# A third step taken ahead in an attention-over-pairs kernel, with the scores of all ahead steps as one run before the first regular step

## The chip, the core and the metric

The kernel runs on one core of a Trainium2 chip. The metric is the device time of one execution in microseconds (us), lower is better, given as the median of several runs.

## What is computed

For 1,024 samples, 33 embedding rows of 128 values each are gathered from 33 tables by `ids`. All 528 pairs of fields are multiplied elementwise, each product goes through a 128x128 attention layer with relu, and its dot product with the sample's own `gnn` vector is the pair's score:

```python
inner = x[:, row] * x[:, col]                       # row, col: all pairs of 33 fields
fm = relu(einsum('bpd,ad->bpa', inner, attn_W) + attn_b)
attn = softmax(einsum('ba,bpa->bp', gnn, fm), axis=1)
out = einsum('bp,bpd->bd', attn, inner) * 100.0
z = concatenate([gnn, out], axis=1)
h = concatenate([z, gnn], axis=1)
h = maximum(h @ W_top1 + b_top1, 0.0)
h = maximum(h @ W_top2 + b_top2, 0.0)
y = h @ W_top3
```

## The kernel before

**Tiles and steps.** The samples form T = 8 tiles of 128, and a tile 32 steps of 4 samples. A pair is a field and a distance of 1 to 16, so with 16 fields repeated at the end (33 + 16) one access pattern gives all 16 x 33 = 528 pairs. A regular step S has 4 x 528 = 2,112 columns, in five chunks of 416 or 424 that fill halves of PSUM slots of two banks.

**Who does what in step S.** DVE multiplies (`product`, L464). ACT rounds a part of the product to fp32r (`round_inner`, L355), and DVE forms the rest (`rest_of_inner`, L470: product minus the rounded part). PE computes `hidden(S)`: the first one to three chunks ("native", L627) as fp32 matmuls, each two records in the trace, the others ("split") as three fp32r matmuls (L634 to L636) that need both parts. ACT applies bias and relu, two chunks to an instruction (L347), into one of three `fm` buffers. Every second step PE runs `reduce_steps` (L673): the scores of two steps, 16 small matmuls (32 records), whose weights put each of four groups of samples on its own 32 columns of the array; they accumulate in one PSUM tile over the whole tile of samples. `reduce_steps` raises `s_red` once per run, and a relu into an `fm` buffer waits until the step three before is reduced.

**The steps ahead.** At the start the 33 gathers of the first tile (GpSimd, L320, in chunks of 8 fields, the fifth of 1) come in one after another. While fields 16 to 32 are still on the way, pairs whose two fields lie among the first 16 (8 distances x 8 fields = 64 pairs) can be done. A step ahead has S < 0 and takes 32 samples at once: 32 x 64 = 2,048 columns, four native chunks of 512. There are two (S = -2, -1), for 64 samples, which are those of the regular steps 0 to 15. These steps, S < SHORT = 16, are "short": 4 x (528 - 64) = 1,856 columns in four chunks of 464. The scores of the two ahead steps (64 matmuls of 64 columns, 128 records) come after hidden(0), as those of any pair of steps do.

**What sets the order.** Each engine runs its own list in program order; there is no scheduler. PE's loop (L740) issues hidden(S), then the jobs of step S (`jobs_of`): transposes of gathered fields (`transpose_x`, L682), the `fields` and `mlp` matmuls of the tile before, and at even S the scores of S-2 and S-1. In step -1 the jobs are the transposes of chunks 2, 3 and 4 of the first tile; those of the next tile stand at steps 18, 20, 22, 24 and 26 of each tile. ACT's loop (L410) issues the first relu of step S, the rounding of step S+2, the other relus, then the evacuations of what was transposed (`evacuate_xt`, L386) and the repeats of the first 16 fields (`repeat`, L376; for the first tile after steps -2 and -1). DVE makes the ahead products, waits for all five evacuations and both repeats, makes product(0), and then in iteration S the rest of step S+1 and product(S+3).

**PSUM slots.** `hidden` pairs of chunks, `x_t`, `fields` and `mlp` units take the slots of a ring of RING = 3 in the order of the list `units` (L121); `claim` (L613) waits until the unit three places before has been taken out. A short step has two hidden units, two full steps have five together, three of them in the even one.

**Queues.** SP stores the gathered rows to DRAM for tile 0 after hidden(1) (L281), then for tile 1, and GpSimd's gathers of a later tile wait for the store of the tile before and for its transposes (L317, L318).

Of the kernel before, what the change touches and what calls it, by code (L numbers as in the profile page):

```python
# [12 lines left out]
def afm_tower(nc, gnn, ids, tables, w1, b1, w2, b2, w3, attn_w, attn_b, out):  # L13
# [4 lines left out]
    K = (F - 1) // 2  # L18
# [5 lines left out]
    ALL = T * STEPS  # L24
# [6 lines left out]


    AHEAD, AHEAD_SAMPLES = 8, 32
    BEGIN = -2
    SHORT = -BEGIN * AHEAD_SAMPLES // GROUPS
    AHEAD_PAIRS = AHEAD * AHEAD
    NEAR = AHEAD * (F - AHEAD)
# [5 lines left out]
    FU = 8  # L43
    XJ = -(-F // FU)
# [12 lines left out]
    def edges(S):  # L57

        if S < 0:
            return list(range(0, AHEAD_SAMPLES * AHEAD_PAIRS + 1, 512))  # L60
        if S < SHORT:
            return list(range(0, LEFT + 1, LEFT // 4))
        return EDGES[S % 2]

    def chunks(S):
        return len(edges(S)) - 1

    SPLIT = max(edges(S)[-1] - edges(S)[NATIVE[S]] for S in range(ALL))
    INNER_BUFS, HI_BUFS, FM_BUFS = 4, 3, 3
# [2 lines left out]
    FIELDS_AT = (7, 10, 13, 16)  # L72
    XT_AT = (18, 20, 22, 24, 26)
    FIRST_REPEAT_AT = {-2: 0, -1: 1}
    MLP_AT = (19, 21, 23)
    QUIET = 2
    MAX_AT, EXP_AT, INV_AT, SCALE_AT, TURN_AT = 1, 2, 2, 3, 4
# [2 lines left out]
    PART_END = [STEPS * (t + 1) for t in range(T - 1)] + [ALL - FN, ALL]  # L80
# [7 lines left out]
    def jobs_of(S):  # L88
        t, s = divmod(S, STEPS)
        jobs = []  # L90
        if s in FIELDS_AT and t > 0:
            jobs.append(("fields", t - 1, FIELDS_AT.index(s)))
        if S == -1:
            jobs += [("x_t", 0, c) for c in range(2, XJ)]
        if s in XT_AT and 0 < t + 1 < T:
            jobs.append(("x_t", t + 1, XT_AT.index(s)))
        if s in MLP_AT and t > 0:
            jobs.append(("mlp", t - 1, MLP_AT.index(s)))
        if S in LAST_FIELDS_AT:
            jobs.append(("fields", T - 1, LAST_FIELDS_AT.index(S)))  # L100
        return jobs


    CHUNK_LIST = [(S, c) for S in range(BEGIN, ALL) for c in range(chunks(S))]
    CHUNK_NO = {chunk: n for n, chunk in enumerate(CHUNK_LIST)}
    PAIR_OF = [CHUNK_LIST[n:n + 2] for n in range(0, len(CHUNK_LIST), 2)]

    def hidden_by(S):

        return CHUNK_NO[S, chunks(S) - 1] + 1  # L110

    def relus_by(S):

        return CHUNK_NO[S, chunks(S) - 1] // 2 + 1

    def pairs_of_steps(S):

        return (S - BEGIN) // 2


    units = [("x_t", 0, c) for c in range(2)]  # L121
    for S in range(BEGIN, ALL):
        units += [("hidden", n, 0) for n, pair in enumerate(PAIR_OF) if pair[0][0] == S] + jobs_of(S)
# [4 lines left out]
    with ctx:  # L128
# [6 lines left out]
        def sem(name):  # L135
            return ctx.enter_context(nc.semaphore(name))
# [62 lines left out]
        s_fm = sem("fm_ready")  # L199
        s_red = sem("two_steps_reduced")  # L200
# [3 lines left out]
        s_repeat = sem("fields_repeated")  # L204
# [9 lines left out]
        s_xt_out = sem("x_t_evacuated")  # L214
# [7 lines left out]
        def slot(unit):  # L222
            return ring[place[unit] % RING]
# [111 lines left out]
        def _(act):  # L335
            def relu(n):
                act.wait_ge(s_hidden, 2 * n + 2)
                for S, c in PAIR_OF[n]:
                    if c == 0 and S - FM_BUFS >= BEGIN:
                        act.wait_ge(s_red, pairs_of_steps(S - FM_BUFS) + 1)  # L340
                (S0, c0), (S1, c1) = PAIR_OF[n]
                wide = edges(S0)[c0 + 1] - edges(S0)[c0]
                at = [S0 % FM_BUFS * COLS + edges(S0)[c0], S1 % FM_BUFS * COLS + edges(S1)[c1]]
                first = fm[:, 0, 0:1]
                dst = bass.AP(tensor=first.tensor, offset=first.offset + at[0],
                              ap=[first.ap[0], [at[1] - at[0], 2], [1, wide]])
                nc.scalar.activation(dst, slot(("hidden", n, 0))[:, :, 0:wide], ACT.Relu,  # L347
                                     bias=attn_b_sb[:, 0:1]).then_inc(s_fm, 1)

            def round_inner(S):  # L350
                act.wait_ge(s_inner, S - BEGIN + 1)
                if S >= HI_BUFS:
                    act.wait_ge(s_hidden, hidden_by(S - HI_BUFS))
                at, end = native_cols(S), edges(S)[-1]
                nc.scalar.copy(inner_hi[:, S % HI_BUFS, 0:end - at], plain[:, S % INNER_BUFS, at:end]).then_inc(s_hi, 1)  # L355
# [17 lines left out]
            def repeat(t, c):  # L373
                act.wait_ge(s_xt_out, XJ * t + c + 1)
                x = xt[:, t % 2]
                nc.scalar.copy(x[:, :, F + FU * c:F + FU * c + FU], x[:, :, FU * c:FU * c + FU]).then_inc(s_repeat, 1)  # L376
# [33 lines left out]
            for S in range(BEGIN, ALL):  # L410
# [9 lines left out]
                for n in out_now[1:]:  # L420
                    relu(n)
                if S in FIRST_REPEAT_AT:
                    repeat(0, FIRST_REPEAT_AT[S])
                for kind, of, c in jobs_of(S):
# [21 lines left out]
        def _(dve):  # L446
            def product(S):
                if S - INNER_BUFS >= BEGIN:
                    dve.wait_ge(s_hidden, hidden_by(S - INNER_BUFS))
                if S < 0:  # L450
                    pieces = [((S - BEGIN) * AHEAD_SAMPLES, AHEAD_SAMPLES, 0, AHEAD, 1, AHEAD)]
                elif S < SHORT:
                    pieces = [(GROUPS * S, GROUPS, AHEAD, F - AHEAD, 1, AHEAD), (GROUPS * S, GROUPS, 0, F, AHEAD + 1, K - AHEAD)]
                else:
                    pieces = [(GROUPS * (S % STEPS), GROUPS, 0, F, 1, K)]
                end = 0
                for sample, samples, field, fields, near, distances in pieces:
                    x = xt[:, S // STEPS % 2 if S >= 0 else 0, sample:sample + samples, :]
                    a, b = x[:, :, field:field + fields], x[:, :, field + near:field + near + fields]
                    a = bass.AP(tensor=a.tensor, offset=a.offset, ap=[a.ap[0], a.ap[1], [0, distances], a.ap[2]])  # L460
                    b = bass.AP(tensor=b.tensor, offset=b.offset, ap=[b.ap[0], b.ap[1], [1, distances], b.ap[2]])
                    begin, end = end, end + samples * distances * fields
                    dst = plain[:, S % INNER_BUFS, begin:end].rearrange("d (g k f) -> d g k f", g=samples, k=distances)
                    last = nc.vector.tensor_tensor(dst, a, b, ALU.mult)  # L464
                last.then_inc(s_inner, 1)
# [14 lines left out]
                nc.vector.tensor_scalar(high, src, 1.0, None, ALU.mult).then_inc(s_blocks, 1)  # L480

            def row_max(p):
                dve.wait_ge(s_red, pairs_of_steps(PART_END[p]))
                nc.vector.tensor_reduce(neg_max[:, 0:1], scores_v, AX.XY, ALU.max, negate=True).then_inc(s_max, 1)

            def invert_sum(p):
# [82 lines left out]
                .then_inc(s_setup, 1)  # L569
            gnn_block(0)  # L570
            dve.wait_ge(s_xt_out, 2)
            product(-2)
            product(-1)
            dve.wait_ge(s_xt_out, XJ)
            dve.wait_ge(s_repeat, K // FU)
            product(0)
            for S in range(BEGIN, ALL):
                t, s = divmod(S, STEPS)
                if 0 <= S + 1 < ALL:
# [32 lines left out]
        def _(pe):  # L612
# [25 lines left out]
            def block_of(s, j):  # L638
                k = min(s, STEPS - 1 - s)
                at = 34 * k if s == k else 33 * k + 32  # L640
                return gnn_blocks[:, j, at - s:at - s + STEPS]
# [17 lines left out]
                        at = j * PAIRS + h * HALF if S >= SHORT else GROUPS * NEAR + j * HALF  # L659
                        yield s, j, s == 0, scores[I * j:I * j + I, h, 0:HALF], fm[:, S % FM_BUFS, at:at + HALF]  # L660

            def reduce_steps(S0, last_pair=False):
                t, s0 = divmod(S0, STEPS)
                if S0 in PART_END:
                    pe.wait_ge(s_exp, PART_END.index(S0) + 1)
                if S0 == BEGIN or s0 == 0:
                    pe.wait_ge(s_blocks, max(t, 0) + 1)
                pe.wait_ge(s_fm, relus_by(S0 if last_pair else S0 + 1))
                for S in (S0, S0 + 1):
                    if last_pair and S > S0:  # L670
                        pe.wait_ge(s_fm, relus_by(S))
                    for s, j, first, to, columns in scores_of(S):
                        last = nc.tensor.matmul(to, block_of(s, j), columns, start=first, stop=S % STEPS == STEPS - 1,  # L673
                                                skip_group_check=True)
                last.then_inc(s_red, 1)
# [64 lines left out]
            for S in range(BEGIN, ALL):  # L740
                hidden(S)
                for kind, of, c in jobs_of(S):
                    if kind == "fields":
                        fields(of, c)
                    if kind == "x_t":
                        transpose_x(of, c)
                    if kind == "mlp":
                        mlp(of, c)
                if S >= BEGIN + 2 and S % 2 == 0:
                    reduce_steps(S - 2)  # L750
            reduce_steps(ALL - 2, True)
            fields(T - 1, 2)
            pe.wait_ge(s_exp, T + 1)
            keep_clock(6)
# [29 lines left out]
```

## Time and profile before

| | |
|---|---|
| median of 3 runs | 1262.59 us (1262.29 to 1263.55) |
| the profiled execution | 1263.74 us |
| its span in the trace | 1261.6 us |
| mean granted TensorE clock | 0.995 of 2.4 GHz |
| the first regular product begins | 52.56 us |

The rows come from the profiled execution. PE is TensorE's matmuls, PEld its weight loads, DVE VectorE, ACT ScalarE, POOL GpSimd, SP the sync engine. In a timeline a row is a start, a duration, the line and operation, output and inputs, how many instructions are merged, and in brackets the idle time before and what ended it. Ends of matmuls are modelled, so successive rows overlap by 0.1 to 0.4 us; distances between starts are the better measure. In the chain of waits, overlaps are taken out. A granted clock of 1.00 is 2.4 GHz, 0.50 is 1.2 GHz.

### The profile page before, as it was taken

What the parts mean: (1) busy time and instruction counts of PE and PEld (TensorE: products, weight loads), DVE (VectorE), ACT (ScalarE), POOL (GpSimd) and SP (SyncE); (2) the same over time, 40 slices, a digit from 0 to 9 for tenths busy, and PEclk for the clock granted to TensorE, in tenths of its full rate; (3) what the DMA queues carried; (4) which work ended last, traced back from release to release, by engine and by line L of the source; (5) the groups of instructions that cost most, each with busy time, mean ns of one, the idle gap of its engine ahead of it and who ended that gap; (6) DMA issues with size and microseconds to landing.
All of it is one profiled execution on the core that took longest, in us unless ns stands there. A gap on an engine that the chain in (4) does not pass through costs nothing.

```text
span 1261.6 us, 20957 instructions
## 1 busy us (share of the span) xinstructions
PE 1203.4 (95%) x8830; PEld 895.1 (71%) x8830; DVE 1144.7 (91%) x667; ACT 1015.3 (80%) x1035; POOL 450.1 (36%) x270
## 2 busy tenths in 40 slices
PE   1699999999999999999999999999999999999998
PEld 1366776777767777777767777677776777777766
DVE  3399899997999989998899989999799998999994
ACT  1488988778887888879887788878888788887883
POOL 6458588028700485006830088102880000000000
PEclk9799999999999999999999999999999999999999
DMA  3121411311113110131101311031110300011001
GB/s 106 28 91 32 122 32 42 113 41 33 32 28 110 32 30 26 30 112 36 30 20 49 103 30 33 18 111 41 30 34 26 112 18 1 1 30 39 18 9 38
DMA packets 54861, 58.86 MB, mean 47 GB/s; under 512 B 10728, under 2 KB 49136, under 8 KB 53744
## 3 DMA queue, kind: packets, MB, share of 16 engines
q1 hardware_dynamic: 46304, 40.20, 10.4%
q0 software_dynamic: 8448, 17.32, 5.2%
q8 instruction: 70, 1.15, 0.4%
q14 instruction: 23, 0.19, 0.0%
q10 hardware_dynamic: 16, 0.00, 0.0%
HBM read 36.12 MB, written 17.31 MB: 42 GB/s over the span
## 4 chain that ended last, share of the span: by engine, by line
PE 85%; ACT 8%; issue 4%; POOL 3%; DVE 1%; DMA 0%; ACTq 0%; DVEq 0%; POOLq 0%
PE scores L673 20%; PE ring L627 18%; PE ring L634 13%; PE ring L636 12%; PE ring L635 12%; PE ring L696 4%; ACT fm L347 3%; POOL x_rows L320 3%; ACT inner_hi L355 2%; PE ring L682 2%; PE ring L716 1%; ACT exp_pairs L362 1%; PE ring L710 1%; PE ring L706 0%; ACT h L394 0%
## 5 line engine op out<-in xcount | busy, mean ns | idle before, releaser
L347 ACT ACTIVATE fm<-ring,attn_b_sb 128x848 f32<-128x848 f32 (+2 forms) x636 | 597.6, 976 | 192.4 <-PE ring L627 177.4
L464 DVE TENSOR_TENSOR products<-xt 128x2112 f32<-128x2112 f32 (+3 forms) x274 | 603.0, 2206 | 33.0 <-ACT xt L386 19.0
L320 POOL DMA_INDIRECT x_rows<-in_tbl,ids_all x264 | 449.4, 1702 | 494.0 <-PE ring L682 377.7
L470 DVE TENSOR_TENSOR low_parts<-products,inner_hi 128x1688 fp32r<-128x1688 f32 (+6 forms) x256 | 462.4, 1806 | 58.6 <-ACT inner_hi L355 57.7
L634 PE MATMUL ring<-inner_hi,attn_wt_lo 128*128 128x424 f32 (+2 forms) x957 | 430.2, 450 | 4.5 <-ACT fm L347 4.5
L355 ACT CAST inner_hi<-products 128x1688 fp32r<-128x1688 f32 (+6 forms) x256 | 388.6, 1518 | 3.9 <-DVE products L464 3.7
L636 PE MATMUL ring<-inner_hi,attn_wt_hi 128*128 128x424 f32 (+2 forms) x957 | 339.8, 355 | 0.0
L635 PE MATMUL ring<-low_parts,attn_wt_hi 128*128 128x424 f32 (+2 forms) x957 | 339.5, 355 | 0.0
L627 PE MATMUL ring<-products,attn_wt 128*128 128x424 f32 (+3 forms) x630 | 285.3, 550 | 11.4 <-DVE products L464 7.8
L673 PE MATMUL scores<-fm,gnn_blocks 128*32 128x264 f32 (+2 forms) x4224 | 255.0, 382 | 6.5 <-ACT exp_pairs L362 6.4
L634 PEld LDWEIGHTS ring<-inner_hi,attn_wt_lo 128*128 128x128 f32 x957 | 180.2, 188 | 70.5 <-issue 39.2
L635 PEld LDWEIGHTS ring<-low_parts,attn_wt_hi 128*128 128x128 f32 x957 | 180.4, 189 | 44.9 <-issue 41.3
L673 PEld LDWEIGHTS scores<-fm,gnn_blocks 128*32 128x32 f32 x4224 | 121.8, 109 | 106.5 <-issue 15.7
L636 PEld LDWEIGHTS ring<-inner_hi,attn_wt_hi 128*128 128x128 f32 x957 | 179.8, 188 | 5.8
L627 PEld LDWEIGHTS ring<-products,attn_wt 128*128 128x128 f32 x630 | 107.4, 191 | 91.7 <-issue 79.0
L696 PE MATMUL ring<-attn_t,x_fields 128*128 128x128 f32 x512 | 62.4, 275 | 1.4 <-ACT attn_t L441 1.4
L696 PEld LDWEIGHTS ring<-attn_t,x_fields 128*128 128x128 f32 x512 | 61.9, 191 | 2.4 <-issue 2.2
L682 PE MATMUL ring<-ident,x_rows 128*128 128x128 f32 x264 | 38.2, 288 | 25.1 <-DMA x_rows<-in_tbl,ids_all 22.1
L386 ACT COPY xt<-ring 128x1024 f32<-128x1024 f32 (+1 forms) x40 | 38.4, 964 | 20.4 <-PE ring L682 17.6
L682 PEld LDWEIGHTS ring<-ident,x_rows 128*128 128x128 f32 x264 | 32.3, 148 | 30.6 <-DMA x_rows<-in_tbl,ids_all 15.8
L520 DVE TENSOR_TENSOR attn<-ring,xt 128x1024 f32<-128x1024 f32 x30 | 36.5, 1217 | 2.1 <-PE ring L696 2.1
L528 DVE TENSOR_REDUCE pooled<-attn 128x32 f32<-128x1024 f32 x30 | 36.4, 1212 | 0.1
(53 smaller groups left out, 203.9 us busy)
## 6 DMA issues: line engine op xcount, KB each, us to landing
x_dram<-x_rows SPq DMA_DIRECT2D x8, 2112.0 KB, 6.7
x_fields<-x_dram SPq DMA_DIRECT2D x128, 128.0 KB
x_rows<-in_tbl,ids_all POOLq DMA_INDIRECT x264
attn_t<-attn_turned SPq DMA_DIRECT2D x124, 32.0 KB
w_sb<-in_W_top SPq DMA_DIRECT2D x2, 512.0 KB
x_fields<-in_r_gnn_feature SPq DMA_DIRECT2D x1, 512.0 KB, 4.2
h<-in_W_top SPq DMA_DIRECT2D x1, 256.0 KB
ids_all<-in_ids SPq DMA_DIRECT2D x1, 132.0 KB, 2.6
```

What stands on the lines that cost most here:

```text
L320: nc.gpsimd.indirect_dma_start(out=x_rows[:, f, :], out_offset=None, in_=tables[f], in_offset=bass.IndirectOffsetOnAxis(ap=ids_all[:, t, f ...
L347: nc.scalar.activation(dst, slot(("hidden", n, 0))[:, :, 0:wide], ACT.Relu, bias=attn_b_sb[:, 0:1]).then_inc(s_fm, 1)
L355: nc.scalar.copy(inner_hi[:, S % HI_BUFS, 0:end - at], plain[:, S % INNER_BUFS, at:end]).then_inc(s_hi, 1)
L464: last = nc.vector.tensor_tensor(dst, a, b, ALU.mult)
L470: nc.vector.tensor_tensor(inner[:, S % INNER_BUFS, at:end], plain[:, S % INNER_BUFS, at:end], inner_hi[:, S % HI_BUFS, 0:end - at].bitcast ...
L627: nc.tensor.matmul(dst, attn_wt[:], plain[:, S % INNER_BUFS, begin:end], start=True, stop=True)\
L634: nc.tensor.matmul(dst, attn_wt_lo[:], hi, start=True, stop=False)
L635: nc.tensor.matmul(dst, attn_wt_hi[:], lo, start=False, stop=False)
L636: nc.tensor.matmul(dst, attn_wt_hi[:], hi, start=False, stop=True).then_inc(s_hidden, 1)
L673: last = nc.tensor.matmul(to, block_of(s, j), columns, start=first, stop=S % STEPS == STEPS - 1, skip_group_check=True)
L682: last = nc.tensor.transpose(to[:, n // 4, n % 4 * P:(n % 4 + 1) * P], x_rows[:, FU * c + n, :], ident[:])
L696: last = nc.tensor.matmul(bank[:, h, to:to + QS * I], x[:, n, :], own[:, :, n, :], start=True, stop=True)
```

## The change

BEGIN becomes -3: three ahead steps, 96 samples. SHORT, computed from it, becomes 24, so regular steps 16 to 23 of the first tile are short too. The transposes of chunk 2 move to step -2, those of chunks 3 and 4 stay at step -1; the repeats stay after steps -2 and -1. `reduce_steps` takes an end: PE issues the scores of steps -3, -2 and -1 as one run (96 matmuls, 192 records) behind the jobs of step -1, ahead of hidden(0), with one increment of `s_red`; regular steps are reduced in pairs as before, and `runs_to` counts these runs. DVE makes all ahead products in a loop; product(0), with its waits, is now the one that the main loop issues at S = -3.

```diff
-    BEGIN = -2
+    BEGIN = -3
@@
     FIRST_REPEAT_AT = {-2: 0, -1: 1}
+    FIRST_XT_AT = {-2: [2], -1: [3, 4]}
@@ jobs_of
-        if S == -1:
-            jobs += [("x_t", 0, c) for c in range(2, XJ)]
+        jobs += [("x_t", 0, c) for c in FIRST_XT_AT.get(S, [])]
@@
-    def pairs_of_steps(S):
-
-        return (S - BEGIN) // 2
+    def runs_to(S):
+
+        return 1 + S // 2 if S >= 0 else 0
@@ relu, on ACT
-                        act.wait_ge(s_red, pairs_of_steps(S - FM_BUFS) + 1)
+                        act.wait_ge(s_red, runs_to(S - FM_BUFS) + 1)
@@ row_max, on DVE
-                dve.wait_ge(s_red, pairs_of_steps(PART_END[p]))
+                dve.wait_ge(s_red, runs_to(PART_END[p]))
@@ DVE
-            product(-2)
-            product(-1)
-            dve.wait_ge(s_xt_out, XJ)
-            dve.wait_ge(s_repeat, K // FU)
-            product(0)
+            for S in range(BEGIN, 0):
+                product(S)
             for S in range(BEGIN, ALL):
@@ PE
-            def reduce_steps(S0, last_pair=False):
+            def reduce_steps(S0, end, last_pair=False):
...
-                pe.wait_ge(s_fm, relus_by(S0 if last_pair else S0 + 1))
-                for S in (S0, S0 + 1):
+                pe.wait_ge(s_fm, relus_by(S0 if last_pair else end - 1))
+                for S in range(S0, end):
@@ PE's loop
-                if S >= BEGIN + 2 and S % 2 == 0:
-                    reduce_steps(S - 2)
-            reduce_steps(ALL - 2, True)
+                if S == -1:
+                    reduce_steps(BEGIN, 0)
+                if S >= 2 and S % 2 == 0:
+                    reduce_steps(S - 2, S)
+            reduce_steps(ALL - 2, ALL, True)
```

## Rows read from the trace of the kernel before

**Rows 1.** The page, part 1: busy us (share of the span) xinstructions.
```profile
PE 1203.4 (95%) x8830; PEld 895.1 (71%) x8830; DVE 1144.7 (91%) x667; ACT 1015.3 (80%) x1035; POOL 450.1 (36%) x270
```

**Rows 2.** The chain that ended last, 0 to 90 us: start us, us, what.
```profile
48.42 2.76 PE ring L682 x9
...
52.56 2.17 DVE products L464 x2
54.77 4.80 PE ring L627 x6
...
60.21 1.92 PE scores L673 x128
...
72.54 0.78 PE ring L627 x2
```

**Rows 3.** Windows: us, busy PE, PEld, DVE, ACT, POOL; clock, DMA share, GB/s.
```profile
41.40:48.40 7.00, 0.00 (x0) 0.00 (x0) 0.00 (x0) 2.37 (x3) 5.21 (x6) 0.80 0.20 53
48.40:50.60 2.20, 2.18 (x9) 1.78 (x9) 0.00 (x0) 0.00 (x0) 0.00 (x0) 0.50 0.10 30
...
54.70:58.90 4.20, 4.13 (x7) 1.95 (x7) 4.20 (x6) 2.17 (x3) 0.00 (x0) 0.50 0.00 0
```

**Rows 4.** Timeline of PE, runs of scores among short steps: start us, us, what.
```profile
67.89 1.78 PE L673 MATMUL scores<-fm,gnn_blocks 128*32 128x200 f32 x32
...
75.15 1.78 PE L673 MATMUL scores<-fm,gnn_blocks 128*32 128x200 f32 x32
...
82.54 1.78 PE L673 MATMUL scores<-fm,gnn_blocks 128*32 128x200 f32 x32
```

**Rows 5.** Timeline of PE, 110 to 160 us: runs of scores, and transposes.
```profile
111.95 1.77 PE L673 MATMUL scores<-fm,gnn_blocks 128*32 128x200 f32 x32
...
119.54 1.78 PE L673 MATMUL scores<-fm,gnn_blocks 128*32 128x200 f32 x32
...
127.52 1.03 PE L682 MATMUL ring<-ident,x_rows 128*128 128x128 f32 x8
128.49 1.99 PE L673 MATMUL scores<-fm,gnn_blocks 128*32 128x264 f32 x32
...
137.65 1.06 PE L682 MATMUL ring<-ident,x_rows 128*128 128x128 f32 x8 [0.78 <-ACT fm L347]
...
157.97 1.99 PE L673 MATMUL scores<-fm,gnn_blocks 128*32 128x264 f32 x32
```

**Rows 6.** Timeline of DVE: ahead products; rest(3), rest(4); a low part at 149 us.
```profile
29.09 4.49 DVE L464 TENSOR_TENSOR products<-xt 128x2048 f32<-128x2048 f32 x2 [13.99 <-issue]
...
66.23 1.61 DVE L470 TENSOR_TENSOR low_parts<-products,inner_hi 128x1392 fp32r<-128x1392 f32 x1 [0.61 <-ACT inner_hi L355]
...
69.83 1.60 DVE L470 TENSOR_TENSOR low_parts<-products,inner_hi 128x1392 fp32r<-128x1392 f32 x1
...
149.18 1.92 DVE L470 TENSOR_TENSOR low_parts<-products,inner_hi 128x1688 fp32r<-128x1688 f32 x1 [0.93 <-ACT inner_hi L355]
```

**Rows 7.** Timeline of GpSimd at the ahead products.
```profile
29.69 2.50 POOL L320 DMA_INDIRECT x_rows<-in_tbl,ids_all  x1 [0.31 <-issue]
32.50 1.90 POOL L320 DMA_INDIRECT x_rows<-in_tbl,ids_all  x1 [0.30 <-issue]
34.71 0.95 POOL L320 DMA_INDIRECT x_rows<-in_tbl,ids_all  x1 [0.31 <-issue]
```

**Rows 8.** Timeline of ACT: evacuation of fields; relus, cast and relu of short steps.
```profile
45.48 1.08 ACT L386 COPY xt<-ring 128x1024 f32<-128x1024 f32 x1 [2.79 <-remote]
...
73.11 1.97 ACT L347 ACTIVATE fm<-ring,attn_b_sb 128x928 f32<-128x928 f32 x2
74.96 1.35 ACT L355 CAST inner_hi<-products 128x1392 fp32r<-128x1392 f32 x1
76.20 1.05 ACT L347 ACTIVATE fm<-ring,attn_b_sb 128x928 f32<-128x928 f32 x1
```

**Rows 9.** Timeline of GpSimd, last gather of the second tile.
```profile
139.45 2.33 POOL L320 DMA_INDIRECT x_rows<-in_tbl,ids_all  x1 [0.30 <-issue]
```
## The prediction

> **What bounds the kernel now.** I read the page first: PE is busy 95% of the span, DVE 91%, ACT 80% [rows 1]. A share that high says that PE work taken off its line is worth its own length wherever PE is the last to be ready, but the change touches only two stretches, so each is read by itself: the start (to about 75 us) and steps 14 to 26 of the first tile (112 to 166 us).
>
> The start is seen in the chain of waits [rows 2]. Up to the landing of the gathers it is GpSimd's chain of gathers; from there nine transposes, two ACT evacuations, product(0) on DVE, the first hidden(0) matmuls at 54.77, and the 128 score matmul records of the two ahead steps, 1.92 us, straight on the chain. The windows [rows 3] show the hole that the change fills: from 41.4 to 48.4 PE has not one matmul, and the chain has it wait from the end of the transposes to 54.77 for product(0). They also show what an idle PE costs: the transposes after the hole run at a granted clock of 0.50 (the 1.2 GHz level), and so does hidden(0), whose three native chunks take to 58.87. After that the clock is full.
>
> In the steady stretch the thing to read is the start of each run of scores, one per two steps [rows 4, 5]. Two short steps (1,856 columns left) take 7.26 us with one native chunk each, 7.39 with a two-chunk step among them [rows 4]. In steps 14 to 26 the same spacing is longer: 7.59 with one short and one full step, 8.95 for the next pair with eight transposes in it, and 29.48 us for the three pairs from 128.49 to 157.97 [rows 5].
>
> **The change, part by part.**
>
> *Third ahead step on DVE.* product(-1) runs right behind the other two, about 33.6 to 35.8 (4.49 us for two, so 2.24 [rows 6]); DVE has nothing else until 52.56. But GpSimd has. Of the gathers then running, the two issued beside the products took 2.50 and 1.90 us, the next, undisturbed, 0.95 [rows 7]: each ended some 0.85 us after a product did. A third product catches the gather issued at 34.71 in the same way: it would end at 35.8 + 0.85 = 36.65 instead of 35.66. I take a delay of 1.0 us for the whole chain of gathers behind it, which is on the path; bounds 0 and 2.25 (the whole product). The Trainium skill says otherwise (SBUF — State Buffer, Who interferes with whom): a tensor_tensor with two SBUF inputs takes only the shared pair's read interface, and descriptor generation was not stalled by one. By that rule this delay would be nothing, and the sum 1.0 us better; the rows, where gathers of 0.95 become 2.50 beside such products, speak against it.
>
> *Third ahead step on PE.* hidden(-1) is four chunks of 512 columns, eight records. A native chunk of 464 columns takes 0.78 us at full rate (the chain at 72.54 [rows 2]), so 512 columns are 0.86 and the step 3.4 us. It follows the transposes of chunk 2, so 41.4 to about 44.9, wholly inside the hole. Its two relus (of 1,024 elements, as the evacuation of 1.08 us) and the evacuation of chunk 2 fit on ACT, which has them done before 50 even though that evacuation ran only at 45.48 [rows 8]. Cost nothing; without that cover, 3.4 us, or 6.9 at the half rate.
>
> *Ahead scores as one run before hidden(0).* 96 matmuls, 192 records, in place of 64 and 128. At 1.92 us for 128 they take 2.9 us at full rate, 5.8 at half. They can start behind the transposes, now at about 51.6 because of the 1.0 above, and hidden(0) can start at 54.77 + 1.0 = 55.8. So they end between 54.5 and 57.4; I take full cover, since PE is now busy from 49.4 on. What goes from the path is the 1.92, and with PE kept at work, hidden(0) meets a higher clock: its three native chunks at 0.78 instead of 1.37 each (4.1 us from 54.77), 1.8 us less.
>
> *What is late next.* PE is not alone there. DVE works from product(0) at 52.56 to the end of rest(4) at 69.83 + 1.60 = 71.4 with one wait, 0.61 us for ACT's cast [rows 6]. With PE ahead, that wait goes (the cast stood behind a relu), but the whole chain shifts by 1.0: rest(4) ends at 71.8. Before, the split matmuls of hidden(4) began at 72.54 + 0.78 = 73.3 [rows 2]. PE's own work from hidden(0) to that place was 73.3 - 54.8 = 18.5 us; less 1.9 and 1.8 it is 14.8, which from 55.8 ends at 70.6, so DVE decides, at 71.8. **The start gains 73.3 - 71.8 = 1.5 us.** Ends: with the half clock kept through hidden(0), 55.8 + 18.5 - 1.9 = 72.4, a gain of 0.9; with the scores also wholly at half rate and hidden(0) at half behind them, 57.4 + 16.6 = 74.0, a loss of 0.7; with no delay of the gathers, 2.5.
>
> *Eight more short steps.* Steps 16 to 23 lose 256 of 2,112 columns each, in hidden, scores, products, casts and low parts. I price them by the spacings that such steps have in the same trace. Transposes of eight fields are 128.49 - 127.52 = 0.97 us.
> - to the scores after step 16: 7.59 becomes 7.26, gain 0.33.
> - after step 18 (17 has two native chunks): 8.95 becomes 7.39 + 0.97 = 8.36, gain 0.59.
> - the three pairs from 128.49 to 157.97: two become 7.26 + 0.97 = 8.23; the third has one short and one full step as the 7.59 pair has, so 8.56. Together 25.02 for 29.48, gain 4.46.
> - after step 26: only the scores of 22 and 23 are narrower; the run of scores is 1.78 instead of 1.99, gain 0.21.
>
> Of the 4.46, some 2.4 is PE's own columns and 2.0 is a stall that should vanish: the transposes at 137.65 wait 0.78 us for a relu [rows 5]. PSUM slots are taken in a ring of three units. In a full even step three hidden units stand before the transposes, so these claim the slot of the first unit of the same step, hardly taken out. A short step has two units, so they claim that of the step before, done long since. ACT must then keep up: per pair four relus at 0.93 (73.11 to 74.96 for two), two casts at 1.24 (74.96 to 76.20), an evacuation and a repeat of 1,024 elements at about 1.08 each [rows 8] are 8.36 us, just above 8.23. I take 8.3 for those two pairs, so 0.1 less. **These steps gain 5.5 us.**
>
> *Waits on other queues.* SP's first store of rows waits for hidden(1), which comes 1 or 2 us earlier; GpSimd's gathers of the second tile follow it. Their last is issued at 139.45 and done at 141.8 [rows 9], and PE wants the last full chunk of fields at about 151 now instead of 157: still covered. The counts of two-step reductions are renumbered and release the same buffers. Later tiles have the same instructions as before.
>
> **Sum.** 1.5 + 5.5 = 7.0 us. Against the profiled execution's own 1263.74 us that is 1256.7. The median shown, 1262.59, lies 1.15 below that execution, so the median should become 1255.6.
>
> **The rivals.**
> - *ACT keeps the pace in steps 18 to 22.* If the claims still wait, the two pairs save only ACT's own work: one relu of 0.86, two casts 0.5, less 0.3 for the wider relus, 1.1 of 10.15 instead of 1.9. Then 5.5 becomes 4.0 and the time is 1257.1. For it: the 8.36 above is close. Against: the slot order.
> - *The start gives nothing.* The clock stays at the half level through scores and hidden(0), or the gathers lose 2.25 us: from a gain of 0.2 to a loss of 0.7, so 1256.9 to 1257.8. The trace shows the low clock after both holes [rows 3], and no hole as short as the new one (44.9 to 49.4). The Trainium skill (TensorE: Matmul & The Clock Gate, Part 4: PE-mode transpose) says that transposes don't count toward the full clock; no row here separates that, but the transposes at 48.42 ran at 0.50.
> - *A better start.* Gathers not delayed, or the clock still full at the transposes, which then take 1.0 instead of 1.9 us: a gain of 1.0 or 1.9 more, 1254.6 or 1253.7.
> - *It does nothing.* The columns only move, and DVE, at over 90% busy, was the pace of steps 16 to 23: 1262.6. Against: DVE still waits there for ACT, 0.93 us at 149.18 [rows 6], and its short steps are cheaper too.
> - *Slower.* hidden(-1) stands behind chunk 2's transposes on PE, and its relus ahead of the last two evacuations on ACT. That ACT evacuated chunk 2 only at 45.48, released by something the profile calls remote [rows 8], is the one sign that it may really be ready later than recorded. If PE started hidden(-1) at 45.4 and at half rate, it would end at 52.2, product(0) would begin at about 56.1 2.5 after the 53.6 of my sum, so the start would lose 1.0; total 1258.1. To be over 2.5 us slower than before, product(0) must come 1.5 + 5.5 + 2.5 = 9.5 us after 53.6, so chunk 2 some 7 us later still; then 1265.1 or more. Chunk 2's gathers are issued long before chunk 3's, whose transposes ran at 48.42, which excludes most of it.
>
> **How the numbers follow.** The sum 0.55; ACT keeps the pace 0.17; no gain at the start 0.13; better start 0.08; nothing 0.04; slower 0.03. The forecast alone spans 1254.7 to 1256.5. The range 1253.7 to 1258.8 takes in the better start, both weaker cases and the mild form of the late chunk. 0.2% (2.5 us) is about what a measurement of this kernel can tell from no change; all cases but the last two lie below 1260.1, with a little of the weaker ones allowed for: faster 0.92, same 0.05, slower 0.03.
>
> **What the profile after should show.** PE busy in about 41.4 to 44.9; one gather near 34.7 of about 1.9 us and chunk 3's transposes near 49.4; 192 score records of 64 columns ending before about 55.8; hidden(0) at a clock above 0.50; DVE without a wait up to rest(4). Scores spaced 7.3 to 8.4 us up to step 22 and no PE wait for ACT before those transposes. From step 26 on all spacings as before. I am wrong if the transposes of chunk 3 come much after 49.4, if scores sit between them and a ready product(0), or if the spacings of steps 18 to 22 stay above 9.

## The result, and the profile after

The changed kernel takes 1268.07 us (median of 6 runs, 1266.41 to 1268.96), the kernel before 1262.72 in the runs beside it: 1.0037 of it, 95% interval 1.0028 to 1.0047. It is 5.3 us slower, where 7.0 faster was forecast, and outside the range. The profiled execution took 1268.51 us, its span is 1266.2, 4.6 more than before.

The page after, its busy line (for [rows 1]), two of its rows in 40 slices of 31.7 us, and the gathers' group:

```profile
PE 1205.8 (95%) x8878; PEld 894.7 (71%) x8878; DVE 1142.8 (90%) x676; ACT 1013.3 (80%) x1033; POOL 476.7 (38%) x270
...
PE   1899799999999999999999999999999999999998
...
POOL 6478858518800386005840088201880000000000
...
L320 POOL DMA_INDIRECT x_rows<-in_tbl,ids_all x264 | 476.0, 1803 | 472.0 <-PE ring L679 370.4
```

The averages say almost nothing: PE and DVE are as busy as before. But GpSimd has nearly 27 us more for the same 264 gathers, and PE has a dip in its fifth slice, 127 to 158 us. (L679 is before's L682, the transposes; L670 is L673, the scores; L624 is L627, the native chunks.)

The timeline of PE at the start:

```profile
41.43 3.60 PE L624 MATMUL ring<-products,attn_wt 128*128 128x512 f32 x8
49.78 2.18 PE L679 MATMUL ring<-ident,x_rows 128*128 128x128 f32 x9 [4.75 <-DMA x_rows<-in_tbl,ids_all]
51.89 4.77 PE L670 MATMUL scores<-fm,gnn_blocks 128*32 128x64 f32 x192
56.59 2.60 PE L624 MATMUL ring<-products,attn_wt 128*128 128x464 f32 x6
...
65.74 1.78 PE L670 MATMUL scores<-fm,gnn_blocks 128*32 128x200 f32 x32
...
73.50 1.78 PE L670 MATMUL scores<-fm,gnn_blocks 128*32 128x200 f32 x32
```

This is the forecast's start. hidden(-1) fills the hole, the transposes come at 49.78, hidden(0) runs at the full clock (1.00 from 56.6 to 59.3; 2.60 us for three chunks instead of 4.1), and the scores after step 4 begin at 73.50 instead of 75.15 [rows 4], 1.65 us earlier. It stays so up to the third set of scores with transposes:

```profile
117.53 1.78 PE L670 MATMUL scores<-fm,gnn_blocks 128*32 128x200 f32 x32
124.82 1.04 PE L679 MATMUL ring<-ident,x_rows 128*128 128x128 f32 x8
125.79 1.78 PE L670 MATMUL scores<-fm,gnn_blocks 128*32 128x200 f32 x32
133.15 1.09 PE L679 MATMUL ring<-ident,x_rows 128*128 128x128 f32 x8
134.17 1.78 PE L670 MATMUL scores<-fm,gnn_blocks 128*32 128x200 f32 x32
150.86 1.97 PE L679 MATMUL ring<-ident,x_rows 128*128 128x128 f32 x8 [9.36 <-DMA x_rows<-in_tbl,ids_all]
152.76 2.79 PE L670 MATMUL scores<-fm,gnn_blocks 128*32 128x200 f32 x32
...
162.65 1.78 PE L670 MATMUL scores<-fm,gnn_blocks 128*32 128x200 f32 x32
```

At 134.17 the kernel is ahead by 4.5 us (its counterpart before began at 138.65). Then PE stands idle for 9.36 us until the third chunk of the second tile's fields is there. After the hole the clock is low for a while (0.50 was granted from 150.8 to 152.8): the same transposes take 1.97 instead of 1.04, the scores 2.79 instead of 1.78. At 152.76 the lead has become a lag of 4.0, and from 162.65 on it stays between 4.5 and 4.7.

The chain of waits leads from there to one gather. It gives the gather only the first 3.13 us and calls the rest issue; GpSimd's timeline (the second block) shows the gather's whole length:

```profile
69.94 3.13 POOL x_rows L320
73.07 28.73 issue
101.80 2.03 POOL x_rows L320
...
147.34 3.47 DMA x_rows<-in_tbl,ids_all
...
150.86 1.97 PE ring L679 x8
```

```profile
32.83 1.90 POOL L320 DMA_INDIRECT x_rows<-in_tbl,ids_all  x1 [0.30 <-issue]
35.03 1.89 POOL L320 DMA_INDIRECT x_rows<-in_tbl,ids_all  x1 [0.30 <-issue]
...
69.94 31.56 POOL L320 DMA_INDIRECT x_rows<-in_tbl,ids_all  x1 [20.52 <-DMA x_dram<-x_rows]
101.80 2.03 POOL L320 DMA_INDIRECT x_rows<-in_tbl,ids_all  x1 [0.30 <-issue]
```

The first gather of the second tile took 31.56 us; in the kernel before, none took over 3.0. It ended at 101.5. DVE's timeline has the first pause of a run of products and low parts there:

```profile
66.15 1.60 DVE L470 TENSOR_TENSOR low_parts<-products,inner_hi 128x1392 fp32r<-128x1392 f32 x1
67.67 2.16 DVE L464 TENSOR_TENSOR products<-xt 128x800 f32<-128x800 f32 x2
69.74 1.60 DVE L470 TENSOR_TENSOR low_parts<-products,inner_hi 128x1392 fp32r<-128x1392 f32 x1
...
98.52 2.16 DVE L464 TENSOR_TENSOR products<-xt 128x800 f32<-128x800 f32 x2
101.40 1.61 DVE L470 TENSOR_TENSOR low_parts<-products,inner_hi 128x1392 fp32r<-128x1392 f32 x1 [0.72 <-ACT inner_hi L355]
```

From product(0) at 53.17 to 100.7 DVE did not pause once. Before, it had waited 0.61 us for ACT at 66.23 [rows 6], and the gather issued 6.8 us later took 1.26:

```profile
73.05 1.26 POOL L320 DMA_INDIRECT x_rows<-in_tbl,ids_all  x1 [24.92 <-DMA x_dram<-x_rows]
```

**Theory L (lockout).** A gather that GpSimd issues into a long unbroken run of DVE operations with two SBUF inputs gets no turn until the run is broken. The early scores make PE early, DVE's pause goes, and with it the gather's turn. Rivals: the gather is slow by itself (its DMA queue, the store ahead of it), or it is the third ahead step.

### The profile page after: what moved, and what is told of

The parts are those of the page before. It is cut to its first block, busy times and chain, and to the rows that moved or that the text cites. A ratio compares the mean times of both kernels' runs of the same rounds, so it can differ in the third digit from the quotient of the medians.

```text
span 1266.2 us, 21064 instructions
## 1 busy us (share of the span) xinstructions
PE 1205.8 (95%) x8878; PEld 894.7 (71%) x8878; DVE 1142.8 (90%) x676; ACT 1013.3 (80%) x1033; POOL 476.7 (38%) x270
## 3 DMA queue, kind: packets, MB, share of 16 engines
q1 hardware_dynamic: 46304, 40.20, 10.5%
## 4 chain that ended last, share of the span: by engine, by line
PE 78%; ACT 7%; issue 7%; POOL 6%; DMA 1%; DVE 1%; ACTq 0%; POOLq 0%; DVEq 0%
PE scores L670 18%; PE ring L624 16%; PE ring L631 12%; PE ring L633 11%; PE ring L632 11%; POOL x_rows L320 6%; PE ring L693 4%; ACT fm L347 3%; ACT inner_hi L355 3%; PE ring L679 2%; PE ring L713 1%; ACT exp_pairs L362 1%; PE ring L707 1%; DMA x_dram<-x_rows 1%; PE ring L703 0%
## 5 line engine op out<-in xcount | busy, mean ns | idle before, releaser
L320 POOL DMA_INDIRECT x_rows<-in_tbl,ids_all x264 | 476.0, 1803 | 472.0 <-PE ring L679 370.4
L470 DVE TENSOR_TENSOR low_parts<-products,inner_hi 128x1696 fp32r<-128x1696 f32 (+6 forms) x256 | 460.2, 1798 | 66.7 <-ACT inner_hi L355 65.8
L355 ACT CAST inner_hi<-products 128x1696 fp32r<-128x1696 f32 (+6 forms) x256 | 386.4, 1510 | 4.6 <-DVE products L464 4.6
L624 PE MATMUL ring<-products,attn_wt 128*128 128x424 f32 (+3 forms) x638 | 287.2, 548 | 7.2 <-ACT fm L347 3.6
L670 PE MATMUL scores<-fm,gnn_blocks 128*32 128x264 f32 (+2 forms) x4288 | 257.9, 383 | 6.5 <-ACT exp_pairs L362 6.5
L670 PEld LDWEIGHTS scores<-fm,gnn_blocks 128*32 128x32 f32 x4288 | 124.9, 112 | 106.7 <-issue 14.4
L624 PEld LDWEIGHTS ring<-products,attn_wt 128*128 128x128 f32 x638 | 108.0, 190 | 87.9 <-issue 79.3
L679 PE MATMUL ring<-ident,x_rows 128*128 128x128 f32 x264 | 39.2, 293 | 31.0 <-DMA x_rows<-in_tbl,ids_all 29.4
L679 PEld LDWEIGHTS ring<-ident,x_rows 128*128 128x128 f32 x264 | 33.0, 151 | 37.5 <-DMA x_rows<-in_tbl,ids_all 24.4
```

Source lines behind the costliest of these rows:

```text
L320: nc.gpsimd.indirect_dma_start(out=x_rows[:, f, :], out_offset=None, in_=tables[f], in_offset=bass.IndirectOffsetOnAxis(ap=ids_all[:, t, f ...
L470: nc.vector.tensor_tensor(inner[:, S % INNER_BUFS, at:end], plain[:, S % INNER_BUFS, at:end], inner_hi[:, S % HI_BUFS, 0:end - at].bitcast ...
L624: nc.tensor.matmul(dst, attn_wt[:], plain[:, S % INNER_BUFS, begin:end], start=True, stop=True)\
L679: last = nc.tensor.transpose(to[:, n // 4, n % 4 * P:(n % 4 + 1) * P], x_rows[:, FU * c + n, :], ident[:])
```

## The experiments

All edits are to the changed kernel except where said.

**e1: one pause.**

```diff
+                    if S + 3 == 6:
+                        dve.wait_ge(s_hidden, CHUNK_NO[4, 1] + 1)
                     product(S + 3)
```

> The changed kernel with one wait added on DVE: product(6) also waits for the second chunk of hidden(4), which ends at about 72.0 us, so that DVE pauses some 0.7 us once, right after the first gather of the second tile has been issued (69.9). Theory L (lockout: a gather issued into a long run of DVE products and low parts without a pause between them gets no turn until DVE pauses): that gather ends at about 73 instead of 101.5, no transposes of the second tile wait for gathers, and the time is the one forecast, 1255 to 1257. Rival Q (the gather is slow by itself, from its DMA queue, the store of rows ahead of it or its code): one pause of DVE changes nothing, the gather still takes about 30 us and the time stays at 1266 to 1269.

Measured 1257.03 us, 0.9951 of before (0.9934 to 0.9967). DVE's timeline has the pause, GpSimd's the gather:

```profile
72.51 2.16 DVE L464 TENSOR_TENSOR products<-xt 128x800 f32<-128x800 f32 x2 [0.99 <-PE ring L635]
```

```profile
70.13 2.21 POOL L320 DMA_INDIRECT x_rows<-in_tbl,ids_all  x1 [20.61 <-DMA x_dram<-x_rows]
```

2.21 us instead of 31.56, and no transposes of the second tile wait for gathers. An added wait of DVE makes the kernel 11 us faster. L stands; the gather is not slow by itself.

**e2: early scores alone** (two ahead steps, in the changed code).

```diff
-    BEGIN = -3
+    BEGIN = -2
-    FIRST_XT_AT = {-2: [2], -1: [3, 4]}
+    FIRST_XT_AT = {-1: [2, 3, 4]}
...
-            for S in range(BEGIN, ALL):
+            for S in range(-3, ALL):
```

(The last edit, in DVE's loop, lets it issue product(0) at S = -3.)

> Two ahead steps as before, but their scores as one run before hidden(0): the second part of the change alone. Theory L: PE gets ahead, the pause of 0.6 us that DVE had at 66 us goes, the first gather of the second tile comes into a run of some 16 us without a pause and is locked out until about 100; the transposes of chunk 2 then wait some 4 us and the time is 1263 to 1266. Rival (it needs the third ahead step): the gather takes 1 to 2 us and the time is the start's gain better than before, 1260 to 1261.

Measured 1271.08 us, 1.0066 (1.0049 to 1.0082). Its gather is locked out as well:

```profile
69.31 30.88 POOL L320 DMA_INDIRECT x_rows<-in_tbl,ids_all  x1 [21.22 <-DMA x_dram<-x_rows]
```

The early scores do it without a third step. The size was missed: I had 4 us of waiting, it was 8.74 (transposes of chunk 2 at 152.79).

**e3: third step alone**, the ahead scores after hidden(0).

```diff
-                if S == -1:
+                if S == 0:
                     reduce_steps(BEGIN, 0)
```

> Three ahead steps, but their scores after hidden(0), where the kernel before has them: the first part of the change alone. Theory L: hidden(0) runs at the half clock again and 2.9 us of scores are on PE's line, so DVE waits for ACT at about 67 to 70 as in the kernel before, the first gather gets in at once, and the time is 1262.7 less 5.5 for the eight shorter steps plus 1 to 2 for the longer scores and the later gathers: 1258 to 1259.5. Rival (the third ahead step itself brings the long gather): 1266 to 1270.

Measured 1260.22 us, 0.9974 (0.9963 to 0.9985): faster than before, 0.7 us above what I gave it. DVE waits for ACT again, for longer than before, and the gather takes its 0.94 us:

```profile
65.48 1.12 DVE L470 TENSOR_TENSOR low_parts<-products,inner_hi 128x928 fp32r<-128x928 f32 x1 [2.90 <-ACT inner_hi L355]
```

```profile
73.68 0.94 POOL L320 DMA_INDIRECT x_rows<-in_tbl,ids_all  x1 [24.59 <-DMA x_dram<-x_rows]
```

So the third step is not what makes the change slow.

**e4: a memset between.** It writes one column of a spare buffer, before each low part of steps 4 to 14 (the buffer's declaration is left out here).

```diff
+                if 4 <= S <= 14:
+                    nc.vector.memset(spare[:, S:S + 1], 0.0)
                 nc.vector.tensor_tensor(inner[:, S % INNER_BUFS, at:end], ...
```

> The changed kernel with a memset of one column (a DVE operation without an SBUF input) before each low part of steps 4 to 14. If the lockout is of the port that two-input operations of DVE share with GpSimd, a single operation that doesn't read SBUF lets the gather in: it ends at 74 to 75 and the time is 1255 to 1257. If only a real pause of DVE does, the gather stays locked out to about 100 and the time is 1266 to 1269.

Measured 1255.73 us (one run). DVE makes no pause, and the gather takes 2.23 us. An operation without an SBUF input breaks the run as well as a pause does.

**e7: a single memset**, `if S == 4`.

> The changed kernel with one memset of one column on DVE before the low part of step 4, about 1 us before the gather is issued. It breaks the run of two-input operations once. Theory L: the gather gets in at the next end of a product, and the whole gain of the change stands: 1255 to 1257, at least as good as the pause of e1, which cost DVE 1 us. Rival (the memset must come while the gather is waiting): locked out, 1266 to 1269.

Measured 1256.47 us (5 runs, 1256.13 to 1256.66), 0.9950 (0.9936 to 0.9963). DVE and GpSimd:

```profile
67.33 2.15 DVE L465 TENSOR_TENSOR products<-xt 128x800 f32<-128x800 f32 x2
69.41 1.60 DVE L473 TENSOR_TENSOR low_parts<-products,inner_hi 128x1392 fp32r<-128x1392 f32 x1
69.43 0.06 DVE L472 MEMSET spare<- 128x1 f32 x1
70.93 2.15 DVE L465 TENSOR_TENSOR products<-xt 128x800 f32<-128x800 f32 x2
```

```profile
69.60 2.23 POOL L321 DMA_INDIRECT x_rows<-in_tbl,ids_all  x1 [20.29 <-DMA x_dram<-x_rows]
```

The gather got its turn at the end of the low part, 70.93, and was done 0.9 us later. This version beats both kernels.

**e11: the same place, but two inputs.**

```diff
-                    nc.vector.memset(spare[:, S:S + 1], 0.0)
+                    nc.vector.tensor_tensor(spare[:, S:S + 1], gnn_t[:, 0:1], gnn_t[:, 1:2], ALU.mult)
```

> As e7, with the one-column memset before the low part of step 4 replaced by a one-column tensor_tensor of two SBUF inputs. If what locks the gather out is an unbroken run of operations with two SBUF inputs, this one continues the run: the gather takes about 30 us, time 1266 to 1270. If any short extra operation, or the wait that it takes off the low part, lets the gather in, it takes about 2 us and the time is 1255.5 to 1257.5.

Measured 1267.08 us (one run), locked out:

```profile
68.54 0.15 DVE L472 TENSOR_TENSOR spare<-gnn_t 128x1 f32<-128x1 f32 x1
68.61 1.60 DVE L473 TENSOR_TENSOR low_parts<-products,inner_hi 128x1392 fp32r<-128x1392 f32 x1
```

```profile
68.85 31.51 POOL L321 DMA_INDIRECT x_rows<-in_tbl,ids_all  x1 [19.72 <-DMA x_dram<-x_rows]
```

Same size, same place, same wait taken off the low part. What differs from e7 is that it reads SBUF, two operands of it; an operation with one SBUF input was not tried in this place. The moment of issue is not the difference: the gathers of e7, of e11 and of the changed kernel were all issued about 0.2 us into a low part. The Trainium skill (SBUF — State Buffer, Who interferes with whom) has such a tensor_tensor contend only with GpSimd's reads and reports a probe in which it did not stall a DMA. Of DVE's 2-port modes it says that whoever issues first holds the shared pair "for the whole instruction". The traces show more than that: the gathers do wait for such operations (1.90 us instead of 0.94), and the wait can outlast one instruction, in the changed kernel's long gather 26 DVE operations that began before DVE's pause.

**e8: early scores alone, with the single memset.**

> Two ahead steps with early scores (e2) and the same single memset. Theory L: the lockout goes and what the early scores are worth by themselves is left, the start's gain without the delay of the gathers by a third product: 1.5 to 2.5 us below the kernel before, 1260 to 1261.5. If the lockout was not all that made e2 slow, it stays above 1263.

Measured 1260.57 us (10 runs), 0.9984 (0.9974 to 0.9993), with that gather at 1.56 us; e2, without the memset, was 10.5 us slower. The lockout was what made e2 slow: without it the time lies where the early scores alone were expected.

**e5, e6, e9, e10, e12: how old may the break be?** Each puts the break ahead of the gather: a wait at product(3) for hidden(1) (e5: its second chunk, e9: its third), at product(2) for the second chunk of hidden(0) (e6), at product(4) for the third of hidden(2) (e10), or the memset before the low part of step 1 (e12). The waits have the form of e1's.

> The changed kernel with the added wait at product(3), for the second chunk of hidden(1): a pause of some 0.4 us at about 61, 8.5 us before the first gather of the second tile is issued. If what counts is how long DVE has run two-input operations without a break when the gather comes, this lies at the edge of what was seen: in the kernel before the gather came 6.8 us after a break, in the run with late scores 8.2, and both got in, while one that came 11.2 us after was locked out. I expect it to get in at once (gather under 3 us, time 1255 to 1257.5). If only a break after the gather's issue frees it, 30 us for the gather and 1266 to 1269.

> The same with the pause at product(2), at about 58, some 11.7 us before the gather. By the length of the run the gather is locked out again: about 30 us, time 1266 to 1270. If any break since the store of rows or since the last gather of the first tile would do, it gets in: 1255 to 1257.5.

> As e5, where the wait turned out to be met already and DVE made no pause, but at product(3) DVE now waits for the third chunk of hidden(1): a real pause of about 1 us that ends near 61.5 to 62, some 8 us before the gather's issue. If the length of the unbroken run decides and lies between the 8.2 us that let a gather in and the 11.2 that did not, it gets in: under 3 us, time 1256 to 1258. If locked out (30 us, 1266 to 1269), the length alone does not decide.

> The same at product(4), waiting for the third chunk of hidden(2): a pause of some 0.5 us that ends near 64.6, some 5 us before the gather's issue. By the length of the run the gather gets in, under 3 us, time 1255.5 to 1257.5. If it is locked out here too, then a pause before the issue is not what let it in in the kernel before (6.8 us after a pause), and the theory has to change.

> As e7, with the memset before the low part of step 1 instead of step 4, about 10 us and 9 two-input operations before the gather's issue. Seen so far: with 8 or more unbroken two-input operations behind it the gather was always locked out, with 5 or fewer never. If that holds for a memset as for a pause, it is locked out: about 30 us, 1266 to 1270. If a memset anywhere before it is enough, it gets in: 1255.5 to 1257.5.

One run each. In e5 the wait was already met and DVE made no pause, so it tells only that an added wait by itself changes nothing (gather 31.54 us, 1267.93 us). In e6 DVE paused 0.24 us. The pauses of e9 and e10, from DVE's timelines:

```profile
62.08 2.16 DVE L464 TENSOR_TENSOR products<-xt 128x800 f32<-128x800 f32 x2 [1.06 <-PE ring L635]
```

```profile
64.27 2.16 DVE L464 TENSOR_TENSOR products<-xt 128x800 f32<-128x800 f32 x2 [1.06 <-PE ring L635]
```

and the gathers of e9 and e10:

```profile
69.92 32.69 POOL L320 DMA_INDIRECT x_rows<-in_tbl,ids_all  x1 [20.57 <-DMA x_dram<-x_rows]
```

```profile
68.99 1.85 POOL L320 DMA_INDIRECT x_rows<-in_tbl,ids_all  x1 [19.93 <-DMA x_dram<-x_rows]
```

| run | break ends | gather issued | two-input operations begun between | gather, us | time, us |
|---|---|---|---|---|---|
| e7 | 69.4 | 69.60 | 1 | 2.23 | 1256.47 |
| e10 | 64.27 | 68.99 | 5 | 1.85 | 1257.68 |
| before | 66.23 | 73.05 | 6 | 1.26 | 1262.72 |
| e3 | 65.48 | 73.68 | 7 | 0.94 | 1260.22 |
| e9 | 62.08 | 69.92 | 8 | 32.69 | 1270.16 |
| e12 | 59.2 | 69.22 | 10 | 31.54 | 1268.12 |
| e6 | 57.88 | 69.97 | 12 | 31.54 | 1267.71 |
| changed | 53.17 | 69.94 | 17 | 31.56 | 1268.07 |

e9 missed: time alone does not decide, since 7.8 us locked it out where 8.2 did not. The count orders this table, with 8 or more always locked out and 5 or fewer never, but it is only a description of these first gathers of the second tile. At 6 or 7 it isn't settled: in the third tile's first gathers of these runs, issued at about 170 us with 6 or 7 operations behind them, some got in at the next end of an operation and some, as the changed kernel's own at 170.99 (6.07 us), waited for the next pause.

Later gathers of the third tile, which the table leaves out, break the count. In e4 two of them are long again, each 0.30 us behind the gather ahead of it:

```profile
202.93 15.78 POOL L321 DMA_INDIRECT x_rows<-in_tbl,ids_all  x1 [0.30 <-issue]
222.42 10.41 POOL L321 DMA_INDIRECT x_rows<-in_tbl,ids_all  x1 [0.30 <-issue]
```

```profile
217.78 1.25 DVE L523 TENSOR_TENSOR attn<-ring,xt 128x1024 f32<-128x1024 f32 x1
231.89 1.25 DVE L523 TENSOR_TENSOR attn<-ring,xt 128x1024 f32<-128x1024 f32 x1
```

When each of the two was issued, DVE had begun only one two-input operation since an operation with a single input. Both ended about 0.9 us after DVE had begun an operation that takes one of its two inputs from PSUM (`ring`), so from SBUF only one: that fits L. But in e8 a gather at 207.87 took 10.31 us, and in e2, e5, e9 and e11 one took 6.2 us, and these got in at the end of a product with no break of the run. So a gather inside a stream can be locked out too, a count of 1 doesn't protect it, and a lockout does not always last until a break. That costs nothing that the times show: e4, with the longest of them, is the fastest run of all. What sets whether a lockout begins is open.

## Why the prediction was wrong

- **The start** was right: hidden(-1) free in the hole, low clock gone from hidden(0), gathers delayed by 1.0 (the third one beside a product took 1.89, as priced), DVE last at step 4. Gain 1.65 us for 1.5 forecast. The 192 score records took 4.77 us, between my two ends, and held hidden(0) until 56.59 instead of 55.8; DVE's chain hid that, as in the text.
- **The eight shorter steps** were right in mechanism and nearly in size. In e7, from the scores after step 4 to those after step 26, the time is 159.30 - 73.16 = 86.1 us for 166.37 - 75.15 = 91.2 before: 5.1 gained for 5.5. The transposes no longer wait for a relu, as the slot order said. The term that was mis-sized is the third pair, 9.39 us for 8.56 (before, with two full steps, it took 157.97 - 148.80 = 9.17): in e7 ACT had no idle time from 135 to 151, and PE waited 0.34 us for its relu at 149.14. That ACT's work is the whole difference is argued, not shown.
- **The step that failed** is in "Waits on other queues": GpSimd's gathers of the second tile "follow" the store, "their last is issued at 139.45 and done at 141.8", "still covered". I moved the gathers with their old durations, at the same place where I had just removed DVE's last pause ahead of them. The text had both halves: "that wait goes", and that gathers beside products end only after one ends. It did not ask who else had used the pause. The runs put in its place a gather of 31.6 us, which cost 11.6 us: 1268.07 against 1256.47 in e7, where one memset takes it away.
- **The rivals.** "Slower" had another mechanism and a chance of 0.03. Without the lockout (e1, e4, e7, e10) the time is 1255.7 to 1257.7, inside the range and 0.1 to 2.1 us above the forecast; the forecast's sum held, and only the lockout was missing from it.
- **The rule of the Trainium skill** (SBUF — State Buffer, Who interferes with whom) on tensor_tensor and descriptor generation was rightly set aside for the rows, but I used it only to price one product (bounds 0 and 2.25 us). What the rows showed, gathers that wait beside products, belonged to every place where the change makes DVE's work denser.

Not tried: what exactly of a gather needs the turn, what decides whether a given gather is locked out, and why the changed kernel's runs spread by 2.5 us where e7's spread by 0.5.

## What to carry to other kernels

An idle gap of an engine can be what another engine gets its turn by: before counting a removed wait as a gain, look at what GpSimd issues near it, and at how long DVE will then run two-input SBUF operations without a break. Where a gather or another DMA of GpSimd starts into such a run, try one operation without SBUF inputs (here a memset of one column, 0.06 us) or a short pause right ahead of it, and look at every gather in the trace after: here it freed the one that mattered, while e4 still had a gather of 15.78 us later on. And durations of gathers measured beside one pattern of DVE's work don't hold for a denser one.

## What the runs showed of the hardware

A single indirect gather, 0.94 us when DVE is idle and mostly 0.94 to 3.0 beside it, took 30.9 to 32.7 us in seven kernels, each time until DVE first paused. Shorter lockouts of 3.9 to 15.8 us are in eleven kernels' traces, some ended by a pause of 0.03 us (the changed kernel's gather at 170.99) or by an operation with one input in PSUM, others by nothing that the traces show. A memset of one column right before it prevented the lockout of the second tile's first gather, a tensor_tensor of one column did not. In the changed kernel PE, after 9.4 us without work, ran its next transposes in 1.97 us instead of 1.04, so a late gather costs more than the wait that the profile shows.
